# Another order of the steps of a tile in the last layer: expert products and the first key and query turns in its middle, the last v product in its tail

## The reference

```
xn = layernorm(x)
qkv = xn @ W_qkv                       # 16 heads of 64: q, k, v
q, k = rotary(q / 8), rotary(k)        # cos, sin of the position
sim = q @ k.T over the own and the preceding window of 128 rows, masked
s = (softmax(sim) @ v) @ W_out
g = silu(sum over the two best experts e of w_e * (xn @ We[e]))
x = x + s * g
```

## Time and profile before

| what | value |
|---|---|
| median of 3 runs | 2545.28 us (2543.22 to 2546.12) |
| the profiled execution's own time | 2545.65 us |
| its span, first to last instruction | 2544.0 us |
| mean granted TensorE clock | 0.958 of full speed |
| busy share of the span | PE 92%, DVE 71%, ACT 59%, POOL 38% |

### The profile page before, as it was taken

How to read it: one execution, slowest core, us unless ns; L and a number is a source line. 1 busy time by engine, 2 the same in 40 slices (tenths; PEclk the granted TensorE clock), 3 DMA queues, 4 the chain that set the end, 5 groups by cost and what they waited for, 6 DMA issues and landing times. The chain is left out here.

```text
span 2544.0 us, 42440 instructions
## 1 busy us (share of the span) xinstructions
PE 2329.7 (92%) x14884; PEld 1481.5 (58%) x14884; DVE 1814.1 (71%) x4382; ACT 1488.3 (59%) x2938; POOL 968.4 (38%) x971
## 2 busy tenths in 40 slices
PE   5879999999999999969977589999999999999998
PEld 4722333333333333248866477777778777777777
DVE  7888888887878787424427677777777777777775
ACT  3525556665656566756534266666666666666665
POOL 3431111111111212124426255555666555555564
PEclk9869999999999999989987699999999999999999
DMA  4770223150505050033327300000000000000000
GB/s 131 228 151 14 29 40 45 27 63 22 65 20 65 20 65 21 7 127 119 137 95 248 116 11 15 15 15 10 13 15 15 15 15 15 15 15 15 12 14 10
DMA packets 139953, 133.08 MB, mean 52 GB/s; under 512 B 48740, under 2 KB 128106, under 8 KB 139747
## 3 DMA queue, kind: packets, MB, share of 16 engines
q1 hardware_dynamic: 107395, 98.01, 16.8%
q10 hardware_dynamic: 26848, 15.73, 2.4%
q0 software_dynamic: 5504, 16.69, 1.8%
HBM read 83.90 MB, written 46.14 MB: 51 GB/s over the span
## 5 line engine op out<-in xcount | busy, mean ns | idle before, releaser
L929 DVE TENSOR_REDUCE a_best<-a_ring 128x1 f32<-128x512 f32 (+3 forms) x1280 | 699.7, 603 | 153.6 <-PE a_ring L736 99.8
L841 ACT ACTIVATE a_probs<-a_pss 128x1024 f32<-128x1024 f32 (+3 forms) x640 | 556.3, 896 | 394.6 <-PE a_pss L783 380.8
L695 POOL TENSOR_SCALAR_AFFINE_SELECT a_probs<-a_probs 128x256 f32<-128x256 f32 x256 | 102.9, 408 | 791.1 <-ACT a_probs L841 789.3
L1808 ACT ACTIVATE w_probs<-w_pss,w_top 128x256 f32<-128x256 f32 x512 | 238.5, 471 | 264.5 <-DVE w_top L1893 164.5
L1644 POOL TENSOR_TENSOR w_probs<-w_probs,w_inv 128x512 f32<-128x512 f32 x256 | 311.5, 1217 | 164.5 <-DVE w_inv L1901 157.2
L1675 PE MATMUL w_psw<-wqkv,w_xr 128*128 128x512 f32 x1152 | 299.8, 397 | 10.3 <-POOL w_xr L1604 10.3
L1893 DVE CUSTOM_DVE_ANT_0 w_pss<-w_pss,w_masks 128x256 f32<-128x256 f32 x512 | 208.6, 449 | 127.0 <-PE w_pss L1706 127.0
L736 PE MATMUL a_ring<-g_kb,g_qa 96*128 96x512 bf16 (+3 forms) x640 | 229.4, 373 | 28.6 <-DVE a_best L929 16.8
L736 PE MATMUL a_ring<-a_kb,a_qa 96*128 96x512 bf16 (+3 forms) x640 | 220.2, 353 | 19.1 <-DVE a_best L929 14.8
L1675 PEld LDWEIGHTS w_psw<-wqkv,w_xr 128*128 128x128 f32 x1152 | 206.3, 191 | 44.9 <-POOL w_xr L1604 10.8
L783 PE MATMUL a_pss<-g_qa,g_kb 99*128 99x512 bf16 (+3 forms) x640 | 219.0, 355 | 2.3 <-DMA g_qa<-a_neg_rows 2.1
(11 more groups left out here) (226 smaller groups left out, 4269.3 us busy)
## 6 DMA issues: line engine op xcount, KB each, us to landing
e_w<-in_w SPq DMA_DIRECT2D x16, 1024.0 KB, 7.9
qk_parts<-p_parts SPq DMA_DIRECT2D x32, 384.0 KB, 3.4
g_qa<-qk_parts SPq DMA_DIRECT2D x96, 64.0 KB, 13.3
a_kb<-qk_parts SPq DMA_DIRECT2D x24, 256.0 KB, 9.1
a_qa<-qk_parts SPq DMA_DIRECT2D x96, 64.0 KB, 13.6
g_kb<-qk_parts SPq DMA_DIRECT2D x18, 256.0 KB, 8.7
v_rows<-p_vout SPq DMA_DIRECT2D x8, 512.0 KB, 4.5
expert_in<-zero POOLq DMA_DIRECT2D x16, 256.0 KB, 4.0
```

The costliest lines, as they stand in the source:

```text
L841: act.activation(probs[:, idx % 4, :, lo:CH], pss[idx % 2][:, :, lo:CH], ACT.Exp).then_inc(exp_done, 1)
L929: vec.tensor_reduce(best[:, i // TC, h * TC + i % TC, k:k + 1], bank[:, 0:keys], X, ALU.max).then_inc(ring_taken, 1)
L1808: ins = act.activation(probs[:, p % 4, e, :], pss[p % 2][:, e, :], ACT.Exp, bias=top[:, e, p:p + 1], scale=-1.0, accum_out=rows[:, e, p:p ...
```

## The change

The list is no longer made from a small rule but written out as a string, `STEP_ORDER`. It holds the same steps, the same number of times, so every engine issues the same instructions in another order. The copy of four pairs (ACT) becomes a step of its own, O0 and O1, so that it can stand elsewhere than at PV3 and PV7. Two waits are rewritten, since the R steps now come as R0, R2, R1, R3: PE's wait before S0 and S4 and DVE's wait in the low part count the R steps in the order of the list.

```diff
+STEP_ORDER = ("S0 W0 S1 N0 W1 S2 N1 W2 QR0 S3 N2 W3 QR1 S4 KR0 T0 KR1 KR2 T1 QR2 N3 S5 QR3 T2 E0 E1 PV0 N4 S6 S7 N5 "
+               "KR3 W4 PV1 KR4 QR4 N6 N7 QR5 T3 E2 PV2 R0 T4 R2 E3 O0 PV3 W5 T5 T6 PV4 KR5 R1 T7 PV5 PV6 R3 PV7 O1 G "
+               "X OUT")
 def window_steps():
-    fillers = {0: [("W", 0)], 1: [("W", 1)], 2: [("W", 2)], 3: [("W", 3), ("QR", 0)],
-               4: [("W", 4), ("QR", 1), ("QR", 2), ("KR", 0)], 5: [("W", 5), ("QR", 3), ("QR", 4), ("KR", 1), ("KR", 2)],
-               6: [("E", 0), ("QR", 5), ("KR", 3)], 7: [("E", 1), ("KR", 4), ("KR", 5)]}
     steps = []
-    for p in range(PAIRS):
-        steps.append(("S", p))
-        if p >= 1:
-            steps.append(("N", p - 1))
-        steps += fillers[p]
-        if p >= 3:
-            steps.append(("T", p - 3))
-        if p >= 4:
-            steps.append(("PV", p - 4))
-    steps += [("N", 7), ("R", 0), ("E", 2), ("T", 5), ("PV", 4), ("R", 1), ("T", 6), ("E", 3), ("PV", 5), ("T", 7), ("R", 2),
-              ("PV", 6), ("X",), ("R", 3), ("PV", 7), ("G",), ("OUT",)]
+    for word in STEP_ORDER.split():
+        kind = word.rstrip("0123456789")
+        steps.append((kind, int(word[len(kind):])) if len(kind) < len(word) else (kind,))
     return steps
...
-                            pe.wait_ge(turn_taken["dve"], 4 * t + 2 * (p // 4) + 2)
+                            pe.wait_ge(turn_taken["dve"], max(turns.emptied(t - 1, ("R", p // 2 + n)) for n in range(2)))
...
-                    elif s[0] == "PV" and s[1] % 4 == 3:
-                        half = s[1] // 4
-                        wait(act, pv_done, PAIRS * t + s[1] + 1)
+                    elif s[0] == "O":
+                        half = s[1]
+                        wait(act, pv_done, PAIRS * t + 4 * half + 4)
...
-                vec.wait_ge(turn_high, 4 * tile + n + 1)
+                vec.wait_ge(turn_high, turns.filled(tile - 1, ("R", n), ("R",)))
```

## The result

| | before | after |
|---|---|---|
| median | 2544.25 us (4 runs, 2541.82 to 2546.12) | 2503.66 us (4 runs, 2502.76 to 2508.0) |
| span of the profiled execution | 2544.0 us | 2502.9 us |
| one tile, first S to first S | 33.38 us | 32.14 us |
| last tile | 30.0 us | 31.3 us |

The ratio is 0.9844, 95% interval 0.9827 to 0.9861: some 40 us faster, where 22 were forecast.

The account below looks back on a forecast made before the run. PE was taken to bound the tile, with one stall. Saving 0.69 (stall) + 0.05 (stepping) - 0.03 (R2's slack) = 0.71 us a tile, times 31 = 22 us, gave a median of 2523 us, range 2512 to 2539.

Parts of the forecast that it names:

- What bounds the tile, and the stall: PE bounds the tile; its wait before R2 for DVE's low part of R1 goes, saving 0.69 us a tile.
- The other engines: DVE, POOL and ACT followed through the new order: no stall of more than a few tenths appears.
- The charge of 0.03: At R2, which needs QR5 from DVE with slack 0.1: 0.03 us a tile charged, 0.3 as bound.
- Rival B: R2 waits on QR5 through DVE and POOL exclusion; only 7 us saved, 2538 us; chance 0.15.
- C: Rival: the wait moves whole to R2 or OUT's second half, stalls 0.7; no difference, 2545 us; chance 0.06.
- D: Rival: DVE's chain from S4 to QR5 is over 0.8 us longer; slower, 2560 or 2600 us; chance 0.08.
- How PE steps: PE's starts in the new order, laid out by old spacings; 0.05 us a tile less taken, bounds -0.3 and +0.4.
- The layout: PE's step starts through one new tile, from the old timeline's spacings: next S0 at 32.4 us.
- 32.70: Length in us of the old tile without its stall: 33.39 - 0.69.
- I take 0.05 less: PE's stepping gains only 0.05 us a tile, since 20 small steps lie in 7 runs before and after.
- The range: 8 in 10 for the new kernel's time: 2512 to 2539 us, its high end from the wait at R2.
- The last tile: Not bound by the stall and has the same work: change taken as 0.

Follow-up runs that it names:

- e1: Kernel before the change with R1 and R2 swapped in its step order: 32.97 us a tile, ratio 0.9946 to the kernel before.
- e5: e3 with PV1 moved up behind PV0, one PV run less: 31.69 us a tile, ratio 0.9785 to the kernel before.
- e6: e5 with PV2 and PV3 together between T4 and R2: 31.49 us a tile, ratio 0.9763 to the kernel before.
- e10: Changed kernel with PV's matmuls at 128 weight columns instead of 64, output not the reference's: 33.52 us a tile, ratio 1.0028 to the kernel before.
- e3: Changed kernel with its tail reordered to one PV run less: 31.80 us a tile, ratio 0.9805 to the kernel before.
- e4: Changed kernel reordered to one PV run and three changes more: 32.75 us a tile, ratio 0.9911 to the kernel before.
- e7: e6 with the last tile in the order of the kernel before: 31.49 us a tile, ratio 0.9762 to the kernel before.
- e9: e7 with E2 and W4 exchanged and QR4 before E2: 31.17 us a tile, ratio 0.9740 to the kernel before.
- e2: e1 with PV before T in three places: 32.78 us a tile, ratio 0.9924 to the kernel before.

## Why the prediction was wrong in size

- *What bounds the tile, and the stall*: right. PE was the bound, the wait of R2 on DVE's low part of R1 went, and nothing took its place. Its size was off: 0.79 us (e1) and not 0.69, since I valued the step behind it by the 0.59 of a PV, where the earlier trace rows had 0.49 for a turn before a turn.
- *The other engines*: right. QR5 ended at 19.75 us for 19.8 laid out, and R2's slack of 0.1 to 0.2 sufficed. The charge of 0.03 wasn't due. Rival B stayed a rival, and came true only in e5, where R2 was moved some 0.25 us earlier; the wait of e6 is another, T5 on the low part of R0. C's and D's mechanisms didn't appear in a full tile.
- *How PE steps*: this is the step that failed. The layout gave 32.4 us for the new tile, 0.3 less than 32.70, and I set it aside for the argument that the 20 small steps lie in 7 runs before and after: "I take 0.05 less". I counted runs of small steps between products. What counts is the runs of PV, 8 before and 7 after, because each of them leaves the 128-column matmuls for the 64-column ones and comes back. Measured, the term is 0.45 us: 1.24 - 0.79. Of that about 0.3 is the PV run (0.33 on the average of e10; 0.34, 0.28 and 0.29 in e3, e4 and e5), and 0.08 is OUT (3.45 to 3.37), whose weight load before waited for ACT's last copy and no longer does. The rest, under 0.1, isn't traced to one place; 0.06 of it may belong to the stall (e1). The layout itself was 0.26 too long, nearly all of it in PV5 to PV7 (2.2 us for 2.5 laid out) and OUT.
- *The range* had 0.3 a tile as the bound of better stepping, from spacings read in an order in which hardly any two like steps stood together. The pairs T T and PV PV stood in no row of before, and for them I took the slower neighbour as the bound; the faster side, that a pair costs less than two singles, I left out. Had I kept the layout's 0.3, the forecast would have been some 8 us lower, 2515, still too high.
- *The last tile* was taken as 0; it cost 1.3 us. In it the clock fell for some 3.5 us, but how much of the 1.3 that is, and whether the order has a part in it, stays open (e7, e9).

In us: 38.5 in 31 tiles (0.79 + 0.45 each), less 1.3, against 31 x 0.71 = 22. The 3.9 us before the first S come on top by chance; without them the time would be some 2507.5, still below the range.

## What to carry to other kernels

Where an engine is busy 98% of the time, its order still has a price: read the starts of neighbouring steps and ask for every pair of kinds what it costs, above all between matmuls of other tile widths, and group those. Before the use that comes back to a bank which a slow engine empties, put enough long work, and let the engine that empties it do that before work nobody waits for. And a layout worked out step by step from rows deserves more trust than a symmetry that would cancel what it says.

## What the runs showed of the hardware beyond that

- A pair of 64-column fp32 matmuls into the two halves of the output partitions takes the time of one of 128 columns: 0.43 us for a PV of 4, against 0.89 (e10).
- A transpose between products costs nothing beyond its own 0.43 us (e4); of the kinds of matmul here only PV is dear to visit.
- The same instructions behind the same pauses can run at the upper clock in one execution and at the lower in another: the last tile of e7 (30.1 us, clock 1.00) and of e9 (32.3 us, clock at 0.50 for some 6.7 us).
